# A graph network's gather counts: packed three to a word for GpSimd, masked for VectorE

## The reference

```python
edge_w = edge_attr @ nn_w.T + nn_b
msg = relu(x[src] * edge_w)
out = x @ root + bias
for r in range(3):
    s = segment_sum(where(edge_type == r, msg, 0), dst)
    cnt = segment_sum(edge_type == r, dst)
    out = out + (s / maximum(cnt, 1)) @ W[r]
```

## Time and profile before

| | |
|---|---|
| median of 3 runs | 4117.41 us (4112.71 to 4118.86) |
| profiled execution, first to last instruction | 4117.9 us |
| relational layer 0 | 2148 to 2722 us of the span |
| relational layer 1 | 2800 to 3374 us |
| relational layer 2 | 3450 to 4028 us |
| register loads in them | DVEq 195 of 20 words, POOLq 75 of 8 words |

### The profile page before, as it was taken

How to read it: one execution, slowest core, us unless ns; L and a number is a source line. 1 busy time by engine, 2 the same in 40 slices (tenths; PEclk the granted TensorE clock), 3 DMA queues, 4 the chain that set the end, 5 groups by cost and what they waited for, 6 DMA issues and landing times.

```text
span 4117.9 us, 112272 instructions
## 1 busy us (share of the span) xinstructions
PE 3104.7 (75%) x28301; PEld 2331.3 (57%) x28301; DVE 2876.4 (70%) x10466; ACT 1533.8 (37%) x4045; POOL 2706.7 (66%) x2886
## 2 busy tenths in 40 slices
PE   6886027777776987777648888897888888888887
PEld 4443015555554565555436666676666667666666
DVE  9998026777776677777667777766777766777777
ACT  1000006777764267777623333212333321333320
POOL 5777747777774377777647777636777745777760
PEclk8777558999998999999969999899999989999988
DMA  3222157888884578888834444314443323444430
GB/s 77 55 57 48 27 162 218 237 237 236 237 230 84 162 228 238 237 237 236 200 108 124 123 120 120 108 58 125 122 120 115 114 73 90 122 119 117 116 105 32
DMA packets 386267, 574.01 MB, mean 139 GB/s; under 512 B 134783, under 2 KB 272433, under 8 KB 386163
## 3 DMA queue, kind: packets, MB, share of 16 engines
q0 software_dynamic: 155264, 442.19, 37.8%
q1 hardware_dynamic: 176106, 123.76, 10.1%
q10 hardware_dynamic: 54794, 6.81, 1.1%
HBM read 531.37 MB, written 41.08 MB: 139 GB/s over the span
## 4 chain that ended last, share of the span: by engine, by line
PE 19%; issue 19%; DVE 16%; DVEq 10%; DMA 10%; POOL 7%; ACT 2%; ACTq 1%; POOLq 0%; SPq 0%
DMA ht<-kv_rows,gidx 6%; PE bank L1210 6%; DVE region L1873 6%; DVEq L728 4%; PE bank L1049 3%; POOL ht L584 3%; PE bank L1197 3%; DVE rings L1854 3%; DMA gring<-kv_rows,gidx 2%; DVE rings L1860 2%; POOL gring L618 2%; PE bank L1124 2%; POOL gring L584 2%; PE bank L1145 2%; PE bank L1157 1%
## 5 line engine op out<-in xcount | busy, mean ns | idle before, releaser
L618 POOL DMA_INDIRECT gring<-h_rows,gidx x1248 | 1201.1, 962 | 464.3 <-issue 317.2
L1210 PE MATMUL bank<-rings 128*128 128x96 f32 x6168 | 914.8, 297 | 247.2 <-DVE region L1873 245.3
L1210 PEld LDWEIGHTS bank<-rings 128*128 128x128 f32 x6168 | 811.0, 205 | 444.8 <-DVE region L1873 406.8
L1281 ACT ACTIVATE rings<-rings 128x512 f32<-128x512 f32 x771 | 485.6, 630 | 1366.2 <-DVE rings L1854 1313.0
L1854 DVE TENSOR_TENSOR rings<-bank,gring 128x256 f32<-128x256 f32 x1542 | 582.4, 420 | 390.1 <-PE bank L1210 195.2
L584 POOL DMA_INDIRECT gring<-kv_rows,gidx x512 | 485.7, 949 | 245.9 <-issue 133.4
L1873 DVE TENSOR_TENSOR region<-region,bank 128x192 f32 x1542 | 540.0, 350 | 131.8 <-PE bank L1210 14.7
L584 POOL DMA_INDIRECT ht<-kv_rows,gidx x512 | 486.2, 950 | 173.7 <-issue 118.4
L1322 ACT ACTIVATE ht<-ht,ntop 128x129 f32<-128x129 f32 x1024 | 413.8, 404 | 287.0 <-DVE ntop L1788 278.4
L1197 PE MATMUL bank<-nnwt,rings 64*128 64x256 f32 x3084 | 491.0, 442 | 39.1 <-DMA rings<-edge_attr_T 39.1
L559 POOL DMA_INDIRECT edge_records<-rings x416 | 408.3, 981 | 151.3 <-issue 148.5
(11 more groups left out here) (257 smaller groups left out, 4095.4 us busy)
## 6 DMA issues: line engine op xcount, KB each, us to landing
rings<-node_in_window_T SPq DMA_DIRECT2D x256, 128.0 KB
rings<-edge_attr_T SPq DMA_DIRECT2D x1548, 16.0 KB
gring<-h_rows,gidx POOLq DMA_INDIRECT x1248
kv_rows<-rows SPq DMA_DIRECT2D x50, 258.0 KB, 2.5
rows<-h_rows SPq DMA_DIRECT2D x75, 128.0 KB
gring<-kv_rows,gidx POOLq DMA_INDIRECT x512
ht<-kv_rows,gidx POOLq DMA_INDIRECT x512
region<-edge_records SPq DMA_DIRECT2D x13, 576.0 KB, 7.0
```

Of the source, the lines that this page charges most:

```text
L618: g.indirect_dma_start(out=gring_r[:, 2 * u + k, :], out_offset=None, in_=h_d[l], in_offset=bass.IndirectOffsetOnAxis(ap=gidx_r[:, half, 2 ...
L1210: ins = pe.matmul(b[:, (2 * k + c) * SEG:(2 * k + c + 1) * SEG], prod[:, slot % RL, (2 * k + c) * P:(2 * k + c + 1) * P], one, start=True, ...
L1281: act.activation(prod[:, slot % RL, :], prod[:, slot % RL, :], ACT.Relu).then_inc(s_msg, 1)
```

## The change

The counts of `free_t` go three to a 32-bit word, 9 bits each, and six words hold the 16 counts of two trips. POOL loads six words at the start of half 0 and none at half 1. In the first trip, where nothing was loaded, it now loads too. Before the waits it takes its count out of the word with a shift and a mask. DVE's count of landed pairs gets a mask of 255; the largest value is 208. The tables get the shifts and the or-operations that pack the counts.

```diff
--- before.py
+++ after.py
@@ -58,6 +58,9 @@
 GT = CT // TU
 GPAIRS = CT // 2
 LAND = 2
+FREEBITS, FREES, LANDMASK = 9, 3, 255
+FREEMASK = (1 << FREEBITS) - 1
+FREEWORDS = 2 * U // FREES + 1
 PITCH = 512
 PACK = 4096
 EP, EJ = 128, 416
@@ -199,7 +202,7 @@
         rec_d = dram("edge_records", (P * PITCH, REC))
         eat_d = dram("edge_attr_T", (CT, ND, P))
         lin_d = dram("edge_ends", (1, (CT + 1) * P))
-        TAB = HALVES * HREC + GPAIRS
+        TAB = HALVES * HREC + GT // 2 * FREEWORDS
         tab_d = dram("job_tables", (1, TAB + 2 * JOBC), I32)
         dlt_d = dram("node_in_window_T", (T, P), BF16)
         kv_d = [dram(f"kv_rows{l}", (NP, KVW)) for l in range(2)]
@@ -353,6 +356,7 @@
         ended_j = made(NW, JOBC // 2, BF16)
         ended_f = made(NW, GPAIRS // 2, BF16)
         winj_f, tilej_f, free_f = made(1, JOBC), made(1, JOBC), made(1, GPAIRS)
+        free_i = made(1, GPAIRS, I32)
         assert table_at[0] <= TU // 2 * KVW
 
         attrs = ht_flat[:, 0:CB * UC * ND].rearrange("p (s m) -> p s m", s=CB)
@@ -587,7 +591,7 @@
 
                 run_steps(g, 0, step)
 
-            free_regs = [g.alloc_register(f"free{u}") for u in range(U)]
+            free_regs = [g.alloc_register(f"free{i}") for i in range(FREEWORDS)]
 
             def relation_gathers(l):
 
@@ -603,14 +607,15 @@
                     last = isinstance(trip, int) and trip == GT - 1
                     if u == 0:
                         g.wait_ge(s_gi, l * GT + trip + 1)
-                        if not first:
-                            g.reg_load(free_regs, free_t[:, bass.ds(trip * U, U)])
+                        if half == 0:
+                            g.reg_load(free_regs, free_t[:, bass.ds(trip * (FREEWORDS // 2), FREEWORDS)])
                     if not (first and u < LAND):
                         landed(0, (u - LAND) % U, trip if u >= LAND else trip - 1)
                     if u == U // 2 and not last:
                         copy_indices(1 - half, trip + 1)
                     if not first:
-                        freed = g.snap(free_regs[u], min_val=1, max_val=RPAIRS)
+                        i = half * U + u
+                        freed = (g.snap(free_regs[i // FREES]) >> (i % FREES * FREEBITS)) & FREEMASK
                         g.wait_ge(s_prod, freed + l * RPAIRS)
                         g.wait_ge(s_sp, freed + l * RPAIRS)
                     g.sem_inc(s_gate)
@@ -734,7 +739,7 @@
                 return eng.snap(sets[slot // (U // 2)][HALF + 2 * (slot % (U // 2)) + k], min_val=0, max_val=TU - 1)
 
             def landed(slot):
-                return eng.snap(sets[slot // (U // 2)][2 * HALF + slot % (U // 2)], min_val=1, max_val=GPAIRS)
+                return eng.snap(sets[slot // (U // 2)][2 * HALF + slot % (U // 2)], min_val=1, max_val=GPAIRS) & LANDMASK
 
             return load, window, place, landed
 
@@ -1644,14 +1649,24 @@
             step(v.tensor_tensor(restart[:, 1:T], tile_w[:, 1:T], tile_w[:, 0:T - 1], ALU.not_equal))
             tell("starts", v.tensor_scalar(start_i[:, :], start_f[:, :], float(E), None, ALU.min))
             step(v.tensor_tensor(tilej_f, iota_t[0:1, :], winj_f, ALU.subtract))
-            step(v.tensor_copy(tab_free, free_f))
+            counts = free_i.rearrange("o (g i) -> o g i", i=2 * U)
+            step(v.tensor_copy(free_i, free_f))
             step(v.tensor_copy(tab_win, winj_f))
             after()
             step(v.tensor_scalar(restart[:, :], restart[:, :], RESTART - KEEP, KEEP, ALU.mult, ALU.add))
             step(v.tensor_scalar(tab_tile, tilej_f, float(CT - 1), None, ALU.min))
-            step(v.tensor_scalar(tab_free, tab_free, 1, None, ALU.logical_shift_right))
+            step(v.tensor_scalar(counts, counts, 1, None, ALU.logical_shift_right))
             step(v.tensor_copy(tab_job[:, :, 0:HALF], tab_win.rearrange("o (h i) -> o h i", i=HALF)))
             after()
+            words = tab_free.rearrange("o (g i) -> o g i", i=FREEWORDS)
+            step(v.tensor_copy(words, counts[:, :, 0::FREES]))
+            after()
+            for i in range(1, FREES):
+                n = len(range(i, 2 * U, FREES))
+                step(v.tensor_scalar(counts[:, :, i::FREES], counts[:, :, i::FREES], i * FREEBITS, None, ALU.logical_shift_left))
+                after()
+                step(v.tensor_tensor(words[:, :, 0:n], words[:, :, 0:n], counts[:, :, i::FREES], ALU.bitwise_or))
+                after()
             tiles = tab_tile.rearrange("o (h i) -> o h i", i=HALF)
             step(v.tensor_scalar(tab_job[:, :, HALF:2 * HALF], tiles, TU - 1, None, ALU.bitwise_and))
             step(v.tensor_scalar(tab_job[:, :, 2 * HALF:HREC], tiles[:, :, 1::2], 1, None, ALU.logical_shift_right))
```

## The result

The changed kernel takes 4205.39 us (median of 4 runs, 4202.94 to 4206.65) beside 4117.39 us for the kernel before (4 runs, 4112.71 to 4118.86). The ratio is 1.0214, with a 95% interval from 1.0200 to 1.0229: 88 us slower. The forecast was 4213 us, its own range 4197 to 4228. The profiled execution has a span of 4202.5 us, 84.6 more than the one before.

The account below looks back on a forecast made before the run. The prediction took DVE's own queue of register instructions to set the pace. From the profiled 4117.9 us, +97 for DVE's mask and -2 for GpSimd's loads gave 4213 us; own range 4197 to 4228, 8-in-10 range 4128 to 4232.

Parts of the forecast that it names:

- What bounds the kernel: In the three relational layers DVE's own queue of register instructions sets the pace, though its arithmetic is busy 71%.
- Part 1: The mask on DVE's count stands alone and parts copy from addition: 108 us, less a tenth, +97 us.
- rival (b): DVE's mask stands alone but swallows the copy: 41 us, nine tenths of it, 4154 us; chance 0.08.
- (a): DVE's mask costs next to nothing, packed or left out: 4118 to 4128 us, say 4123; chance 0.13.
- The tenth taken off for other waits: Share of the mask's 108 us on DVE expected to lie beside real waits and stretches where PE sets the pace.
- Part 2: GpSimd's 75 loads of eight words become 39 of six at 0.44 us: 30 us of queue freed, -2 us counted.
- Part 3: GpSimd's unpacking adds up to 124 us to POOL's queue, costed at nothing because it hides behind the gathers.
- (d): POOL becomes the pace through its unpacking, on top of a slower DVE: about 18 us more, 4231 us; chance 0.04.
- Part 4: Five more small table operations, some 2 us at 403 us, hidden by DVE's later wait for the edge records.
- Rival (c): POOL's register loads hold back the landings DVE waits for, so fewer loads make it faster: 4094 us; chance 0.09.
- three signs of "wrong": L737 still one instruction a pair; layer 0 growing as much as the others; L1854's waits naming POOLq L599 over 45 times.

Follow-up runs that it names:

- f3: The changed kernel with a maximum with 1 in place of the mask on DVE's count, packing kept: 4130.80 us, ratio 1.0040 to the kernel before.
- f2: The kernel before with DVE's mask alone; GpSimd's count gets only a maximum with 1, nothing packed: 4205.07 us, ratio 1.0220.
- e3: The same kernel as f3, run where the kernel before takes 5004.60 us: 5015.48 us, ratio 1.0024.
- e4: e3 with the six words of each group starting at multiples of eight words: 5014.92 us beside 5004.60 for the kernel before, ratio 1.0015.

## Why the prediction was right

- **What bounds the kernel.** It held. DVE's arithmetic was no argument (busy 71% of a layer), its queue between the instructions was. All of the loss stands in the gap from the last accumulation to the next multiply (87.2 of 88 us).
- **Part 1, the form.** It held to the instruction: MOVE x771 and ALU_OP x1285, as forecast. The copy was not dropped, so rival (b) fell, and the mask was not packed, so (a) fell. There was luck in it: the reason given was that only copies, additions and address products had been seen packed. By the same reason a maximum would have been put alone, at some 100 us, and f3 shows it packed, at 17.
- **Part 1, the size.** Here the sum was off. A lone register instruction was taken at 0.087 us. It costs 0.077 in layer 0, and the step of layers 1 and 2 is 0.144 instead of 0.167. The 0.087 was 0.04 + 0.05 of issue, read at a single instruction that had another kind behind it; between two operations of one line the chain has 0.03 of issue. With the measured prices 257 x 0.077 + 514 x 0.144 = 93.8 us instead of 108. The tenth taken off for other waits held in the sum: nine tenths of 93.8 are 84.4, and the layers grew by 85.3. By layer it did not: layer 0 grew by 21.8 us, more than its 19.8, and the others by 31.7 of their 37.0. So the forecast of 20 us for layer 0 was met and that of 39 for each of the others too high. Of the 97 us of this term 12 were too many.
- **Part 2.** The count held (39 loads), the price did not: 0.806 us instead of the estimated 0.44, since a load is not paid by the word. Instead of 30 us the queue was spared 36 x (0.567 + 0.065 + 0.05) - 39 x (0.806 - 0.567) = 15 us. No gain shows, as f2 and the changed kernel differ by 0.02 us (with some 4 us of noise); the -2 us of the sum was 0 within that. The prediction had cited the Trainium skill here, page "DMA: Bandwidth & Descriptors", section "Latency and other measured facts", with its floor of about 600 ns for a register load. The trace has eight words slightly below it, at 0.567 us. Six words at 0.806 are above a floor and don't contradict one, but they cost more than eight, which neither the page nor the estimate had foreseen.
- **Part 3.** Half right. The upper bound was chosen, three more instructions a pair in layers 1 and 2; in fact the shift was packed and only mask and addition stand alone: 375 + 225 + 1000 = 1,600 instructions at L618 and L619, fewer than the 2,000 to 2,200 forecast. That the gathers hide it was right (0.14 us before a pair's first gather, and waits for DVE of 1.59 us behind), so (d) fell.
- **Part 4.** Hidden in the wait for the edge records, as said.
- **Rival (c).** It would have shown in f3, the packing without the mask. f3 is 17 us slower than before, not 24 faster, and without the maximum's 15 us it would still not be faster.
- **The signs.** One of the three signs of "wrong" appeared, POOLq named more than 45 times, and it was a false alarm: f2 shows 65 with GpSimd's loads untouched. The sign had been badly chosen, for the prediction itself had said that these waits were DVE's own queue.

The forecast of 4213 us was 8 us over the 4205.39 measured, the sum of 12 too many in part 1, 2 too few in part 2, and 2 outside: the medians differ by 2.7 more than the layers grew, and the sum was made from 0.5 above the median.

## What to carry to other kernels

Before an instruction is added to an engine's queue, look where the queue's work can be seen from the engine: here the queue has to wait for one accumulation to end before it can send the next, and behind that point it is no longer ahead of its engine, so that each lone register instruction made the next multiply 0.07 us later. Written ahead of that wait, where the queue ran in front of the engine, the same instruction added nothing. Look also at what the queue packs (in these kernels an addition, a maximum or a shift joined the copy beside it, the mask did not and even parted the copy from its addition), and judge by start times rather than by the name of a wait, which changes when the engine's own queue is later by a tenth of a microsecond.

## What was not expected of the hardware

- The price of a load into registers does not go by its words alone: 8 words 0.567 us, 20 words 1.352, 6 words 0.79 to 0.82. Starting each group of six at a multiple of eight words changed little (0.809 in e3, 0.792 in e4). The step from 8 words to 20 is 0.785 us, an estimate of 0.26 for each four words (though the 8 are GpSimd's and the 20 VectorE's); by it six words cost about what twelve would. Why isn't shown, and only these three sizes were measured.
- A maximum is packed on DVE's queue (f3: FUSED_REGOPS, 70 ns with copy and addition), a mask is not (f2: three instructions, MOVE 36 and ALU_OP 45 ns). On POOL's queue the shift is packed, the mask is not.
- The same program takes 4114 us in one set of runs and 5005 or 4993 in others. The mask costs 2.2% in the first and 0.5% in the second, and an edit that brings 1.5% in the first was part of a kernel that lost 0.6% in the third. A verdict holds for the chip, and the condition of the chip, on which it was found.
